# A mixture of experts computed for chosen pairs only: places from prefix sums, rows moved by indirect DMA

## The reference, cut to what matters

```
m = _layernorm(x, ln2_g, ln2_b)
xt = m.reshape(-1, Dd)                                    # 2048 x 128
probs = jax.nn.softmax(xt @ Wg, axis=-1)                  # 8 experts
wts, idx = jax.lax.top_k(probs, K)                        # K = 2
wts = wts / jnp.sum(wts, axis=-1, keepdims=True)
h1 = jax.nn.gelu(jnp.einsum('td,edf->etf', xt, W1) + b1[:, None, :])      # 128 -> 512
ye = jnp.einsum('etf,efd->etd', h1, W2) + b2[:, None, :]                  # 512 -> 128
sel = ye[idx, jnp.arange(T)[:, None], :]
moe_out = jnp.sum(wts[..., None] * sel, axis=1).reshape(Bb, Ss, Dd)
return x + moe_out
```

## Time and profile before

| | us |
|---|---|
| median of 3 runs | 3081.71 |
| lowest and highest | 3079.64, 3089.95 |
| the profiled execution, its own time | 3089.07 |
| its span in the trace | 3087.4 |

### The profile page before, as it was taken

One profiled execution on the slowest core, in us unless ns is written; L12 is line 12 of the kernel. 1 busy time (PEld: TensorE's weight loads), 2 busy tenths in 40 slices (PEclk: granted clock), 3 DMA queues, 4 the chain that ended last, 5 costly groups with the idle time before them and its releaser, 6 DMA issues. The chain is left out here.

```text
span 3087.4 us, 50997 instructions
## 1 busy us (share of the span) xinstructions
PE 2811.2 (91%) x15207; PEld 1321.3 (43%) x15207; DVE 2016.6 (65%) x2997; ACT 1746.3 (57%) x3339; POOL 260.1 (8%) x488
## 2 busy tenths in 40 slices
PE   6788856999999999899599999949999999998998
PEld 2688853433333333444244444424333333334443
DVE  5544457788888883322478888747888888872222
ACT  4222211677777787443236776722877777775443
POOL 1222202000000000000111111220000000000000
PEclk9888855899999999899779999966999999998999
DMA  1000002110111100111111111020110111100111
GB/s 39 1 0 0 0 1 75 29 28 17 25 28 28 28 19 3 63 62 41 62 37 35 40 41 41 22 75 14 29 26 17 27 28 28 27 8 14 69 61 34
DMA packets 37080, 94.16 MB, mean 31 GB/s; under 512 B 9258, under 2 KB 23044, under 8 KB 28804
## 3 DMA queue, kind: packets, MB, share of 16 engines
q1 hardware_dynamic: 33892, 91.18, 10.9%
q10 hardware_dynamic: 3104, 1.88, 0.2%
HBM read 78.45 MB, written 13.76 MB: 30 GB/s over the span
## 5 line engine op out<-in xcount | busy, mean ns | idle before, releaser
L509 DVE TENSOR_REDUCE Fmaxes<-Fm 128x1 f32<-128x1024 f32 x512 | 603.4, 1220 | 100.4 <-PE Fm L273 98.9
L509 DVE TENSOR_REDUCE Hmaxes<-Hm 128x1 f32<-128x1024 f32 x512 | 603.4, 1220 | 99.2 <-PE Hm L273 97.7
L420 ACT ACTIVATE Fprob<-Fs 128x512 f32<-128x512 f32 x1024 | 528.5, 604 | 118.1 <-PE Fs L285 117.6
L420 ACT ACTIVATE Hprob<-Hs 128x512 f32<-128x512 f32 x1024 | 528.5, 604 | 117.9 <-PE Hs L285 117.4
L285 PE MATMUL Fs<-Fqa,Fka 64*128 64x512 f32 x1024 | 409.2, 466 | 5.8 <-ACT Fprob L420 5.2
L285 PE MATMUL Hs<-Hqa,Hka 64*128 64x512 f32 x1024 | 409.0, 466 | 5.9 <-ACT Hprob L420 5.4
L905 ACT ACTIVATE Lprob<-Ls 128x512 f32<-128x512 f32 (+3 forms) x640 | 301.7, 542 | 127.3 <-PE Ls L786 126.5
L273 PE MATMUL Fm<-Fka,Fqa 64*128 64x512 f32 x1024 | 350.4, 460 | 19.6 <-DMA Fka<-F_kparts 15.9
L273 PE MATMUL Hm<-Hka,Hqa 64*128 64x512 f32 x1024 | 350.2, 460 | 18.6 <-DMA Hka<-H_kparts 14.9
L273 PEld LDWEIGHTS Fm<-Fka,Fqa 64*128 64x128 f32 x1024 | 162.1, 195 | 277.1 <-DVE Fmaxes L509 252.9
L273 PEld LDWEIGHTS Hm<-Hka,Hqa 64*128 64x128 f32 x1024 | 161.9, 195 | 275.9 <-DVE Hmaxes L509 253.0
(11 more groups left out here) (448 smaller groups left out, 2997.3 us busy)
## 6 DMA issues: line engine op xcount, KB each, us to landing
Fqa<-F_qparts SPq DMA_DIRECT2D x64, 128.0 KB
Fka<-F_kparts SPq DMA_DIRECT2D x64, 128.0 KB
FEwb<-FE_weights SPq DMA_DIRECT2D x8, 1024.0 KB, 5.8
Lqa<-L_qparts SPq DMA_DIRECT2D x64, 128.0 KB
Lka<-L_kparts SPq DMA_DIRECT2D x64, 128.0 KB
Hqa<-H_qparts SPq DMA_DIRECT2D x64, 128.0 KB
Hka<-H_kparts SPq DMA_DIRECT2D x64, 128.0 KB
HEwb<-HE_weights SPq DMA_DIRECT2D x8, 1024.0 KB, 5.5
```

The lines of the kernel that those rows point to most:

```text
L420: nc.scalar.activation(prob[:, kt % PSLOTS, q0:q1], seat(kt, n)[:, 0:q1 - q0], ACT.Exp, scale=SCALE).then_inc(expd, 1)
L509: nc.vector.reduce_max(maxes[:, qt, half:half + 1], mps[j % 2][:, 0:width], AX.X)\
```

## The change

`experts` and `project_add` are replaced by `experts_sorted`. There are 4096 chosen pairs of a token and an expert. Every pair gets a place in a list in which the pairs of one expert stand together and each expert begins at a multiple of 128. Whatever the choice is, 2 x 16 + 8 - 1 = 39 tiles of 128 places are enough, and all 39 are computed.

The places: VectorE marks the chosen experts (`hot`, `chosen`), sums along the tokens of a partition with a scan (`upto`), and TensorE sums over the partitions with a triangle of ones (`earlier`) and a matrix of ones. From an expert's count come its number of tiles, its first tile, and for every pair its place `pos`, split into tile (shift by 7) and rank in the tile (mask of 127). To turn the list round (from pair-to-place to place-to-pair), `tile` and `rank` are one-hot masks, and 32 matmuls, one for 128 pairs, put the pair's number and its weight at [rank, tile] (`tps`). Places with no pair get a spare row and weight zero. `owner` is the expert of each tile.

The tokens n2, normalized but not scaled, are written to HBM (`m_d`). For each tile GpSimd gathers 128 rows of it by an indirect DMA (`gather`); TensorE transposes them (`turn`); VectorE scales by ln2_g and adds ln2_b while it copies (`take`); `raise_` makes four matmuls of 128 columns against W1 of the tile's expert, which SyncE loads for every tile, with the expert's number read from SBUF into a register; ScalarE makes four gelus of 128 columns; `lower` makes four accumulating matmuls with the hidden units as weights and W2 (all of it stands in SBUF) as the moving operand, at a column that a register gives; VectorE multiplies by the pair's weight; and GpSimd scatters the 128 rows to HBM (`scatter`), each to the row of its pair in `y_d`. Four slots (KEEP) of gathered rows, W1 and outputs are used in turn. The order on TensorE in iteration k is: register load, raise k+1, turn k+2, lower k. The order on GpSimd is: gather k+4, scatter k.

The part of b2 (weights times b2) is four matmuls of 512 columns, added to x ahead of the tiles. GpSimd adds n1 to x at the start. At the end all of `y_d` is loaded back in 8 DMAs, and VectorE adds both chosen outputs of every token to x.

```diff
-def experts(nc, name, mT, wg, w1_d, b1T, w2_d, b2T, accT, consts):
...
+TILES = 2 * NT + E_N - 1
+SPARE = 2 * T
+KEEP = 4
...
+def experts_sorted(nc, name, m, mT, wg, w1_d, b1T, w2_d, b2_d, gain, bias, x, n1, consts, moves, turn_no):
...
+        DVE_STEPS = (["mx", "lg", "sm", "rc", "prob"] + [("big", t) for t in range(NT)] + [("idx", t) for t in range(NT)]
+                     + ["idf", "hot", "chosen", "upto", "ahead", "over", "ntile", "ends", "first", "place", "part", "pos",
+                        "posi", "a", "b", "b4", "ab", "val", "s2", "r2", "wj", "tile", "pair0", "pair1"]
+                     + [("rank", q) for q in range(NB)]
+                     + ["before", "owner", "own", "own512", "weigh0", "wts", "rows", "tokens", "wtab",
+                        "owned", "spread", "b1s"])
+        at = {n: k + 1 for k, n in enumerate(DVE_STEPS)}
+        FILLED = 5
...
+                sp.dma_start(m_d.rearrange("(t p) c -> p t c", p=P), m[:, :, :]).then_inc(kept, 16)
+                sp.dma_start(w2[:, :, :], w2_d.rearrange("e (k p) c -> p (e k) c", p=P)).then_inc(w2_in, 16)
+                sp.wait_ge(filled, FILLED)
+                for t in range(NT):
+                    sp.dma_start(b2s[t * E_N:(t + 1) * E_N, t // 4, t % 4, :], b2_d).then_inc(b2_in, 16)
+                sp.wait_ge(step, at["own"])
+                for k in range(TILES):
+                    s = k % KEEP
+                    e = sp.value_load(ownint[0:1, 0, k:k + 1], min_val=0, max_val=E_N - 1)
+                    if k >= KEEP:
+                        sp.wait_ge(up, k - KEEP + 1)
+                    sp.dma_start(w1[:, s, :], w1_d[bass.ds(e, 1), :, :].rearrange("o c f -> (o c) f")).then_inc(w1_in[s], 16)
+                for s in range(KEEP):
+                    sp.wait_ge(y_out[s], moved_at(s, len(range(s, TILES, KEEP))))
+                for b in range(NB):
+                    for j in range(TOP):
+                        sp.dma_start(back[:, j, 4 * b:4 * b + 4, :],
+                                     y_d[j * T + b * BANK:j * T + (b + 1) * BANK, :].rearrange("(t p) c -> p t c", p=P))\
+                            .then_inc(back_in[b], 16)
...
+                nc.gpsimd.memset(ones[:, :], 1.0).then_inc(filled, 1)
+                nc.gpsimd.memset(keep[:, :, :], 1.0).then_inc(filled, 1)
+                nc.gpsimd.memset(b2s[:, :, :, :], 0.0).then_inc(filled, 1)
+                pool.wait_ge(filled, 3)
+                nc.gpsimd.memset(keep[:, :, 0:1], 0.0).then_inc(filled, 1)
+                nc.gpsimd.tensor_tensor(x[:, :, :], x[:, :, :], n1[:, :, :], ALU.add).then_inc(filled, 1)
+
+                def gather(k):
+                    s = k % KEEP
+                    if k >= KEEP:
+                        pool.wait_ge(turned, k - KEEP + 1)
+                    nc.gpsimd.indirect_dma_start(xs[:, s, :], None, m_d[:, :],
+                                                 bass.IndirectOffsetOnAxis(rows[:, 1, k:k + 1].bitcast(U32), 0))\
+                        .then_inc(x_in[s], 16)
+
+                def scatter(k):
+                    s = k % KEEP
+                    pool.wait_ge(scaled, k + 1)
+                    nc.gpsimd.indirect_dma_start(y_d[:, :],
+                                                 bass.IndirectOffsetOnAxis(rows[:, 0, k:k + 1].bitcast(U32), 0),
+                                                 ys[:, s, :], None).then_inc(y_out[s], 16)
+
+                pool.wait_ge(kept, 16)
+                pool.wait_ge(step, at["tokens"])
+                for k in range(KEEP):
+                    gather(k)
+                for k in range(TILES):
+                    if k + KEEP < TILES:
+                        gather(k + KEEP)
+                    scatter(k)
...
+                def turn(k):
+                    s = k % KEEP
+                    pe.wait_ge(x_in[s], moved_at(s, k // KEEP + 1))
+                    if k >= 2:
+                        pe.wait_ge(taken, k - 1)
+                    nc.tensor.transpose(xps[k % 2][:, 0:P], xs[:, s, :], consts["ident"]).then_inc(turned, 1)
+
+                def raise_(k):
+                    s = k % KEEP
+                    pe.wait_ge(w1_in[s], 16 * (k // KEEP + 1))
+                    pe.wait_ge(taken, k + 1)
+                    if k >= 3:
+                        pe.wait_ge(gelu, (k - 2) * FC)
                     for f in range(FC):
-
-                        if not (first and k == 0):
-                            pe.wait_ge(gelu, (i * PAIR_ITEMS + k - 1) * FC + f + 1)
-                        nc.tensor.matmul(hps[f][:, :], w1[:, u, f * P:(f + 1) * P], mT[:, b * BANK:(b + 1) * BANK],
-                                         start=True, stop=True).then_inc(up, 1)
-
-                def lower(i, k, first=False):
-                    u, b = divmod(k, NB)
-
-                    back = YSLOTS if k >= YSLOTS else PAIR_ITEMS + k - max(range(k, PAIR_ITEMS, YSLOTS))
-                    if not (first and k < YSLOTS):
-                        pe.wait_ge(scaled, i * PAIR_ITEMS + k - back + 1)
+                        last = nc.tensor.matmul(hps[k % 3][:, f * P:(f + 1) * P], w1[:, s, f * P:(f + 1) * P],
+                                                xg[:, k % 2, :], start=True, stop=True)
+                    last.then_inc(up, 1)
...
+                def lower(k, e):
+                    if k >= 2:
+                        pe.wait_ge(scaled, k - 1)
                     for f in range(FC):
-                        pe.wait_ge(gelu, (i * PAIR_ITEMS + k) * FC + f + 1)
-                        last = nc.tensor.matmul(yps[k % YSLOTS][:, :], w2[:, u, f, :], hid[:, k % 2, f, :],
+                        pe.wait_ge(gelu, k * FC + f + 1)
+                        last = nc.tensor.matmul(yps[k % 2][:, 0:C], hid[:, k % 2, f, :],
+                                                w2[:, :, :].rearrange("p k c -> p (k c)")[:, bass.ds(e + f * C, C)],
...
+                pe.wait_ge(filled, FILLED)
+                pe.wait_ge(step, at["upto"])
+                nc.tensor.matmul(cps, ones[:, :], upto[:, :, NT - 1], start=True, stop=True).then_inc(ranked, 1)
+                pe.wait_ge(step, at["ahead"])
+                nc.tensor.matmul(rps, consts["earlier"], chosen[:, :, :], start=True, stop=False)
+                nc.tensor.matmul(rps, ones[:, :], ahead[:, :, :], start=False, stop=True).then_inc(ranked, 1)
+                pe.wait_ge(step, at["pair1"])
+                for q in range(NB):
+                    pe.wait_ge(step, at["rank", q])
+                    for n in range(q * 8, q * 8 + 8):
+                        last = nc.tensor.matmul(tps, rank[:, n, :], pair[:, n, :, :], start=(n == 0), stop=(n == 2 * NT - 1))
+                last.then_inc(tabled, 1)
+                pe.wait_ge(step, at["wts"])
+                nc.tensor.transpose(wps, wts[:, :, :].rearrange("p t e -> p (t e)"), consts["ident"]).then_inc(wt, 1)
+                pe.wait_ge(b2_in, 16 * NT)
+                pe.wait_ge(wt_sb, 1)
+                for b in range(NB):
+                    nc.tensor.matmul(b2ps[b][:, :], wT[:, :], b2s[:, b, :, :].rearrange("p t c -> p (t c)"),
+                                     start=True, stop=True).then_inc(b2_made, 1)
+                pe.wait_ge(step, at["b1s"])
+                turn(0)
+                turn(1)
+                pe.wait_ge(b2_added, NB)
+                pe.wait_ge(w2_in, 16)
+                raise_(0)
+                for k in range(TILES):
+                    e = pe.value_load(ownint[0:1, 1, k:k + 1], min_val=0, max_val=(E_N - 1) * FC * C)
+                    if k + 1 < TILES:
+                        raise_(k + 1)
+                    if k + 2 < TILES:
+                        turn(k + 2)
+                    lower(k, e)
...
+                act.wait_ge(wt, 1)
+                nc.scalar.activation(wT[:, :], wps, ACT.Copy).then_inc(wt_sb, 1)
+                act.wait_ge(step, at["b1s"])
+                for k in range(TILES):
+                    if k >= 2:
+                        act.wait_ge(down, k - 1)
+                    act.wait_ge(up, k + 1)
+                    for f in range(FC):
+                        nc.scalar.activation(hid[:, k % 2, f, :], hps[k % 3][:, f * P:(f + 1) * P], ACT.Gelu_apprx_tanh,
+                                             bias=b1s[:, k, f:f + 1]).then_inc(gelu, 1)
...
+                nc.vector.tensor_tensor_scan(flat(upto), flat(keep), flat(chosen), 0.0, ALU.mult, ALU.add).then_inc(step, 1)
+                need("upto")
+                nc.vector.tensor_tensor(ahead[:, :, :], upto[:, :, :], chosen[:, :, :], ALU.subtract).then_inc(step, 1)
...
+                    n = slice(q * 8, q * 8 + 8)
+                    nc.vector.tensor_tensor(rank[:, n, :], consts["count"].unsqueeze(1).broadcast_to([P, 8, P]),
+                                            ab[:, 1, n].unsqueeze(2).broadcast_to([P, 8, P]), ALU.is_equal)\
+                        .then_inc(step, 1)
...
+                dve.wait_ge(tabled, 1)
```

(85 more changed lines are left out.)

251 lines of the change are left out of this document (117 added, 134 removed).

## The result

| | before | after |
|---|---|---|
| median, us | 3082.06 (4 runs, 3079.64 to 3089.95) | 2933.60 (4 runs, 2925.46 to 2933.83) |
| profiled execution, us | 3089.07 | 2933.82 |
| its span, us | 3087.4 | 2931.6 |

The ratio of the times is 0.9508, 95% interval 0.9484 to 0.9531: the kernel is faster by 148 us. The forecast was 2988 (94 us), and the time lies inside the range of 2900 to 3150. But it lies outside the band that the forecast gave itself (2957 to 3027): it is 54 us from the forecast and 16 from the first rival (2918).

A forecast was written before the change was run, and what follows sets the result against it. PE bounds the old expert stage, 236.2 us, run twice. New stage 60.5 + 39T, T = 3.3 with POOL's DMAs and a partly low clock: 189, saving 47, twice 94; forecast 2988 us, range 2900 to 3150.

The forecast's parts named there:

- the first rival: Tile loop: indirect DMA 1.0 us or less, PE nearly without gaps at the high clock, T = 2.4; 2918 us; chance 18%.
- a third of the loop at the low clock: Tile loop: two thirds at 3.0 us a tile, one third with PE cold at 4.0, giving T = 3.3.
- T: Period of one tile in the expert stage's loop, taken as 3.3 us; break-even at 4.5 us.
- loop, 39T + 3: 39 tiles of period T, plus 3 us for the pipeline to fill and drain, in each new stage.
- The start: New stage up to the first expert matmul: DVE chain, table matmuls, first gather, b2; first raise at +42.5, between +41 and +46.
- the price of an indirect DMA: POOL's time per gather or scatter, taken as 1.4 us with the index read; two per tile, 3.0 with waits.
- The low stretch at 500 us: Profiled stretch before the change where PE waits for DVE between pairs and its clock stays at 0.50 for forty microseconds.
- PE stays low: Rival for the tile loop: gaps and register loads keep the clock at 0.50, T = 4.2; 3058 us; chance 12%.
- POOL slower than before: Rival for the tile loop: indirect DMAs hold POOL over 2.2 us each, T exceeds 4.5, the change loses; chance 28%.
- The ring of latencies: Tile loop: scatter waits for scaled(k), then gather(k+5), needed five tiles later; T = 2.3, not bounding unless issues cost far more.
- The end: End of the stage: scatter issue and landing, 2 MB back in eight loads (10 us), two last additions; 15 us in sum.
- The register loads: Expert-number loads on SP and PE per tile, in no profile row; bounded by nothing to 1.8 us, 0.2 taken on PE.

The follow-up runs named there:

- idle-matmul kernel: Changed kernel plus seven wide matmuls with unread results on TensorE ahead of the table matmuls in each stage; 2918.20 us, ratio 0.9455.
- plain stores: Changed kernel with each stage's 39 scatters replaced by plain 64 KB stores from SyncE to consecutive rows (pairs' rows land wrongly); 2886.70 us, one run.
- plain loads: Changed kernel with each stage's 39 gathers replaced by plain 64 KB loads of consecutive rows from SyncE (tiles get wrong tokens); 2886.52 us, one run.
- the third indirect DMA: Changed kernel plus one more indirect gather per tile on GpSimd, into a buffer nothing reads; 3023.68 us, one run.
- half gather: Changed kernel with gathers fetching 64 rows, not 128, from the fifth tile on; 2932.56 us, one run.

## Why the prediction was right, and where it was off

The sign and the range hold, and so does half of the mechanism: PE waits for POOL or for gathered rows, one period a tile, and POOL's issues stand under 1.4 us apart. The other half, a third of the loop at the low clock, did not happen. Of the signs that the prediction named for being right, the loop of about 129 us and a clock between 0.6 and 0.95 failed in the first stage (98.4 us, 1.00). And a range of 250 us, from T = 2.2 to 5.4, holds some 85% of the outcomes by the prediction's own chances, so lying inside it says little. Step by step, for the first stage:

| term | predicted | measured |
|---|---|---|
| first table matmul | +23.8 | +23.0 |
| 32 table matmuls | 12 | 13.9 |
| first raise | +42.5 (41 to 46) | +45.0 |
| an indirect DMA on POOL, with its wait | 1.5 | 1.28 |
| PE's work on a tile, high level | 2.1 | 1.9 |
| clock in the loop | a third of it low | 1.00 |
| loop, 39T + 3 | 131.7 | 98.4 |
| last scaling to end | 15 | 14.7 |
| stage | 189 | 158.1 |

**The start** was late for the reason given as its upper bound: the table matmuls run at the low level, at 13.91/64 = 0.217 us a record, about twice the 7.34/64 = 0.115 of the idle-matmul kernel. b2 (two groups, 5.4 us and the last pair) sets the first raise. The DVE chain came out as summed. `spread` alone was mispriced: 2.38 us, where the masks of the same 1248 elements take 1.46 as predicted; it lies beside b2 and cost nothing at four slots, where POOL waits for the first scaled tile anyway (3.66 us; 4.81 when the gather came without `spread`). With eight slots POOL has no such wait, so there the 2 us that the first gather lost beside `spread` are on the path; an order that sets them apart was not tried with eight slots.

**The loop** is where the forecast failed, by 33.3 us: the period T. It had two mis-sized terms. First the price of an indirect DMA, the one resource without a row: 1.0 us and a fixed gap of 0.30 ahead of it, not 1.4 and a wait; two of them a tile are 2.57, not 3.0, which is 0.43 x 39 = 17 us. The loop taken by the sum's formula gives T = (98.4 - 3)/39 = 2.45; the other 0.12 x 39 = 5 us come from the gathers issued ahead of the first raise, which the sum did not take off. Second the clock: I gave a third of the loop to the low level, which took T from 3.0 to 3.3, 0.3 x 39 = 12 us. It stayed at 1.00, with 661 records in 99 us, and even with 222 in 50 it was 0.94. The low stretch at 500 us, which I used as the other end, has 17 records in 10 us and was no neighbour. With the measured price alone in T, the forecast's own sum is 60.5 + 39 x 2.57 = 161 us, against 158.1.

**Between the first rival and the forecast.** The first rival asked for issues of 1.0 us or less and PE without gaps, T = 2.4. The time is near its 2918, but not by its mechanism: at 0.97 + 0.30 a DMA, POOL still bounds. The plain stores and plain loads, with which PE does bound, give 1.90 us a tile and about 2887. The rival's T was right by two errors: PE's tile was taken at 2.1, not 1.9, with 0.3 of gaps on top, and POOL was thought out of the way.

**The other rivals.** PE stays low: the clock row of the loop says no. POOL slower than before: the third indirect DMA gives the slope, 1.25 us of POOL for each more; the loss would need 4.5 us a tile, between three (3.80) and four of them. The rule named in the prediction from the Trainium skill (DMA: Bandwidth & Descriptors, Latency and other measured facts), a first byte after about 1 us from GpSimd, is near to the 0.97 and 0.99 us that an instruction holds POOL here, although that is another quantity, and it leaves out the gap of 0.30, which is what keeps POOL the bound.

**The ring of latencies** (T = 2.3 by the prediction, so hidden) held: eight slots do not change the steady period of 2.57. They change the ends. POOL's waits for the first scaled tile (3.66 and 3.93 us), for some of the last, and after late gathers were not in the prediction's sum; they are 5.7 and 11.3 us in the two stages.

**The end** came out to 0.3 us. From the issue of the first return load (1409.90) to the end it is 11.7 us for 10 and two additions; the loads of 256 KB land after 5.0 us:

```profile
FEw<-in_L_ffn_W SPq DMA_DIRECT2D x39, 256.0 KB, 2.8
FEback<-FE_chosen SPq DMA_DIRECT2D x8, 256.0 KB, 5.0
```

**The register loads,** for which I took 0.2 us on PE and bounded 1.8: with plain stores or loads the period is 1.90 us and PE is busy for 50.00 of 50 us (the plain loads, from 1320 to 1370), so they cost nothing that can be seen.

## What to carry to other kernels

A resource that the trace of before does not show (here a kind of instruction on an idle engine) deserves the whole range between its nearest rows, and the count of its instructions on the path is worth more than their bytes: here 64 rows fewer in each gather saved nothing, and one instruction a tile out of POOL's queue took 21 us from a loop. Read such a kernel's loop on the engine that bounds it, from its first instruction to its last; its waits at the two ends are what a deeper ring takes away. And if an engine must wait before a burst of small matmuls, work with no use ahead of it can pay: it nearly halved the 19.3 us of the table matmuls and the first of b2.

## What was not expected of the hardware

- An indirect DMA holds POOL for 0.97 us (gather) or 0.99 (scatter) for 128 rows of 512 bytes, 0.91 for 64 rows, and has 0.30 us ahead of it; a plain one of the same 64 KB takes 0.58 and 0.04.
- The first gather took 3.08 us beside a VectorE tensor_tensor with both inputs in SBUF, and 1.17 when the two were set apart; 3.10 and 1.16 in the two kernels with idle matmuls and four slots. The prediction's rule on stopped descriptors (the Trainium skill, SBUF — State Buffer, Who interferes with whom) speaks of copies and tensor_scalar. Of a tensor_tensor the same section says that with both inputs in SBUF it contends with GpSimd's reads, but that a probe did not see it stall a DMA; this indirect gather lost 2 us beside one. The scalings in the loop left no such mark: POOL's gathers and scatters in the steady loop are 0.97 and 0.99.
- A VectorE tensor_tensor over three free dimensions, both operands broadcast and one of them permuted, took 2.38 us for 1248 elements, other shapes of as many elements 1.46.
- Three gathers of 39 in the second stage landed after 4.1 to 4.4 us, where the others landed in time (2.52 in the chain of the kernel without W1 loads). They come and go between executions: five other kernels with four slots and both indirect DMAs had no wait of POOL behind a late gather in that stage, four of them with all their W1 loads, while the half gather has such a wait in its first stage (1.48 us at 1324.77). Why those three stays open.
